# Eight shared-expert tasks in front of the routed tasks, none among them

## The chip, the cores and the metric

The kernel runs on one core of a Trainium2 chip. The metric is the time of one execution on the device in microseconds (us); the median of three runs is given. Matrix products run on TensorE (PE), elementwise work on VectorE (DVE), activations and copies on ScalarE (ACT), small operations and gathers and scatters by index on GpSimd (POOL), and most plain transfers are issued by SyncE (SP) and ScalarE.

## What is computed

One transformer layer over a batch of two sequences of 1,024 tokens, width 256: attention and then a mixture of experts, each behind a layer norm and with a residual.

```python
x = x + attention(layernorm(x))          # 16 heads of 128, causal
x = x + ffn(layernorm(x))

def ffn(x):                              # 2,048 tokens
    topk_idx, topk_w = route(x)          # sigmoid scores; 4 of 8 groups, 8 of 32 experts
    for g, u, d, c in 32 experts:        # inner size 128
        out += c[:, None] * ((silu(x @ g.T) * (x @ u.T)) @ d.T)
    shared = (silu(x @ shared_gate.T) * (x @ shared_up.T)) @ shared_down.T    # inner size 256
    return out + shared
```

Each token uses 8 of the 32 routed experts, and every token uses the shared one.

## The kernel before

The first 940 us are attention, for both sequences (batch 0 and batch 1), in head pairs; while the second half of it runs, the tokens of batch 0 are normalized and routed, and their rows are written to a buffer `xs` in device memory, sorted by expert, in tiles of 128 rows. Every expert gets at least one tile; each batch has room for 96 tiles, and tiles behind the last used one are computed as tiles of the last expert in the order. Products are split into three of reduced precision each (a high and a low part; lines 824 to 826, helper `three`).

The experts' work is a fixed list of 112 **tasks**, built by `dealt()`. A *routed* task ("m") is two tiles of sorted rows, 48 for each batch (routed tasks 0 to 47 are batch 0, from 48 on batch 1); a *shared* task ("s") is 128 tokens through the shared expert, 8 for each batch. Before the change the order is: shared 0 to 3 of batch 0, routed 0 to 26, shared 4, routed 27 to 34, shared 5, routed 35 to 42, shared 6, routed 43 to 50, shared 7, routed 51 to 95, and the 8 shared tasks of batch 1. A task's position in the list is called g. So routed task 27 stands at g = 32, 40 at 46, 42 at 48, 52 at 60; from routed task 51 on, g is the task's number plus 8.

All engines go through the same list of items, written by `step_items(n)`. Step n is: A, the gate and up products of task n + 2 (`gate_up`, 12 products a task, lines 824 to 826); E, if task n + 4 is routed, the transposes of its rows (`transpose_rows`, L1016); B, the transposes of the hidden values of task n + 1 (L1028); C, the down products of task n (`down`, L1047). A shared task has no E: its rows are the tokens, which are in SBUF already, and its weights are there too. TensorE handles the items in exactly this order, so an A that waits holds everything behind it.

The first 36 steps (`after_attention`) also hold batch 1's second normalization half (items N, and the transposes Y), the router's logits (L, M), routing (G) and slots (K), two to a step for the first 20 steps and one after that, put in at places 1 and 3 of each step's list. An E that isn't there moves what is behind it one place forward.

Weights of the routed experts come through a **ring** of 8 places. SyncE loads expert e (512 KB of split gate and up weights, 128 KB of down weights) into place e mod 8 as soon as the tiles of expert e - 8 have been computed:

```python
if e >= RING:
    until_done(0, e - RING)      # waits on s_y, which counts computed tiles
load(e % RING, e, wanted)        # two transfers, L569 and L570
if e > 0:
    relay(0, e - 1)              # L565: waits for e - 1 to land, then s_w += 1
```

An expert between 8 and 23 without tokens is skipped. TensorE's `gate_up` waits until `s_w` says that the weights of the task's second tile are there. Batch 1 goes through the experts in reverse order, 31 first, and starts with the eight that batch 0 left in the ring; its first new load needs its own first tile computed.

Other transfers in this stretch: ScalarE loads the sorted rows, 512 KB for two routed tasks, four pairs ahead, and stores the results of two tasks in the same way (512 KB). GpSimd scatters the rows of batch 1 to their sorted places: 64 scatters of 128 rows of 1 KB, of which scatter i waits for task g = 15 + i // 2 to be done; then it gathers result rows for batch 0 and 1, in 128 gathers, each pair behind one more task (from g = 47 on). These gates go by the position g, not by the routed task's number. VectorE adds a shared task's output to the tokens' sum (L1592) and splits off low parts (L1595 for rows, L1344 for normalized tokens); the rows of a token are added with their weights from step 62 on.

Of the kernel before, what the change touches and what calls it, by code (L numbers as in the profile page):

```python
# [97 lines left out]
NEWTON = range(NC, B * NC + 2)  # L98
NS = B * NT
NTASK = NS + B * PT  # L100
LEAD, DEALT_BEHIND = 4, (26, 34, 42, 50)
NSH = SI // I
TAIL = 36
COMBINE = NT + PT + 6
# [1620 lines left out]
```

## Time and profile before

| | |
|---|---|
| median of 3 runs | 1325.95 us (1322.28 to 1327.79) |
| the profiled execution | 1325.1 us, of which the span from first to last instruction is 1323.4 |
| instructions | 28,678 |
| TensorE busy in the span | 1285.6 us (97%) |
| VectorE, ScalarE, GpSimd busy | 884.5, 736.3, 571.5 us |
| mean granted TensorE clock | 0.994 of full speed |
| start of the first shared task's gate-up | 944.5 us |

Times in the rows are counted from the start of the span. A profile's timeline merges like instructions that follow each other: "1.03 PE L1047 ... x4" are four products that take 1.03 us from the first one's start to the last one's end. What stands in brackets behind a row is the engine's idle time just before it and what ended it. Matmuls overlap, so the time of a step is best read from start to start.

### The profile page before, as it was taken

How to read it: one execution, taken by the hardware profiler on the slowest of the kernel's cores; microseconds unless marked ns; L12 is line 12 of the kernel's file. 1: busy time of each engine (PE TensorE's matmuls, PEld its weight loads, DVE VectorE, ACT ScalarE, POOL GpSimd, SP SyncE). 2: the span in 40 equal slices, each digit the busy share in tenths (PEclk: the TensorE clock that was granted, in tenths of full speed). 3: DMA queues.
4: the chain of work that ended last, by engine and by line, in shares of the span. 5: the costliest groups of instructions: out<-in, count | busy, mean ns of one | idle time of the engine just before them, and what ended most of it. 6: DMA issues, size and time to landing. Idle time of an engine off the chain costs nothing.

```text
span 1323.4 us, 28678 instructions
## 1 busy us (share of the span) xinstructions
PE 1285.6 (97%) x8324; PEld 1154.0 (87%) x8324; DVE 884.5 (67%) x2120; ACT 736.3 (56%) x1660; POOL 571.5 (43%) x675
## 2 busy tenths in 40 slices
PE   7999999999999999999999999999999998999998
PEld 6898888988888897879888888988789998899996
DVE  5666666776766969687777766676767532356645
ACT  3656555565555655455555555555556664566653
POOL 3636445364430414132244537363000764666674
PEclk8999999999999999999999999999999999999999
DMA  3252645525362001010001112011268998999973
GB/s 125 88 183 89 208 135 182 184 97 182 122 222 99 18 16 29 5 28 19 19 29 61 44 62 69 26 51 57 64 223 290 305 318 297 316 317 389 366 236 115
DMA packets 124796, 188.18 MB, mean 142 GB/s; under 512 B 10016, under 2 KB 97824, under 8 KB 124704
## 3 DMA queue, kind: packets, MB, share of 16 engines
q1 hardware_dynamic: 61024, 101.91, 23.2%
q10 hardware_dynamic: 51392, 51.52, 11.9%
q0 software_dynamic: 12288, 33.57, 7.3%
q8 instruction: 52, 0.85, 0.3%
q14 instruction: 40, 0.33, 0.1%
HBM read 107.79 MB, written 87.03 MB: 147 GB/s over the span
## 4 chain that ended last, share of the span: by engine, by line
PE 79%; DVE 7%; issue 7%; ACT 4%; DMA 3%; SPq 0%; ACTq 0%; POOL 0%; DVEq 0%; POOLq 0%
PE ps_t L879 8%; PE ps_s L824 7%; PE ps_s L826 7%; PE ps_s L825 7%; PE ps_x L824 6%; PE ps_x L826 5%; PE ps_x L825 5%; PE ps_z L824 4%; PE ps_z L826 4%; PE ps_z L825 4%; PE ps_t L1047 3%; PE ps_z L1047 3%; PE ps_s L1016 3%; PE ps_t L824 2%; PE ps_t L826 2%
## 5 line engine op out<-in xcount | busy, mean ns | idle before, releaser
L1170 ACT ACTIVATE prob<-prob,neg_max 128x128 f32<-128x128 f32 (+7 forms) x256 | 198.6, 776 | 244.0 <-DVE neg_max L1370 243.8
L1391 DVE TENSOR_TENSOR pT_lo<-ps_t,pT_hi 128x512 fp32r<-128x512 f32 (+2 forms) x320 | 189.8, 604 | 101.3 <-ACT pT_hi L1185 98.7
L1185 ACT ACTIVATE pT_hi<-ps_t 128x512 fp32r<-128x512 f32 (+2 forms) x320 | 161.5, 532 | 86.3 <-PE ps_t L879 86.3
L1370 DVE CUSTOM_DVE_ANT_0 prob<-ps_s,later_keys 128x128 f32<-128x128 f32 (+7 forms) x256 | 186.1, 749 | 1.9 <-PE ps_s L826 0.8
L879 PE MATMUL ps_t<-ident,prob 128*128 128x128 f32 x1152 | 170.9, 273 | 8.1 <-ACT prob L1170 6.0
L719 POOL DMA_INDIRECT xs<-xn,slots x128 | 125.5, 981 | 123.0 <-DVE slots L1538 53.3
L879 PEld LDWEIGHTS ps_t<-ident,prob 128*128 128x128 f32 x1152 | 136.5, 140 | 33.4 <-issue 6.1
L824 PE MATMUL ps_s<-k_hi,q_hi 128*128 128x512 f32 (+2 forms) x384 | 140.9, 367 | 0.9 <-DVE k_lo L1363 0.9
L1583 DVE TENSOR_TENSOR h<-sg,ps_s 128x256 f32<-128x256 f32 x112 | 47.1, 421 | 137.2 <-ACT sg L1219 137.0
L824 PE MATMUL ps_s<-ring,a_hi 128*128 x384 | 126.4, 329 | 7.3 <-SPq L565 7.0
L634 POOL TENSOR_TENSOR a_hi<-raw_a,zero 128x512 fp32r<-128x512 f32 x30 | 31.2, 1040 | 236.0 <-PE ps_x L826 194.3
L826 PE MATMUL ps_s<-k_hi,q_lo 128*128 128x512 f32 (+2 forms) x384 | 131.9, 344 | 0.0
L825 PE MATMUL ps_s<-k_lo,q_hi 128*128 128x512 f32 (+2 forms) x384 | 131.6, 343 | 0.0
L824 PE MATMUL ps_z<-pT_hi,v_hi 128*128 128x512 f32 (+2 forms) x320 | 122.5, 383 | 1.6 <-DVE pT_lo L1391 1.6
L826 PE MATMUL ps_z<-pT_hi,v_lo 128*128 128x512 f32 (+2 forms) x320 | 115.7, 361 | 0.0
L825 PE MATMUL ps_z<-pT_lo,v_hi 128*128 128x512 f32 (+2 forms) x320 | 114.9, 359 | 0.0
L826 PE MATMUL ps_s<-ring,a_lo 128*128 x384 | 109.5, 285 | 0.0
L1406 DVE SCALAR_TENSOR_TENSOR acc<-ps_t,inv_sum,acc 128x256 f32<-128x256 f32 x256 | 108.7, 477 | 0.2 <-PE ps_t L826 0.2
L825 PE MATMUL ps_s<-ring,a_hi 128*128 x384 | 108.5, 282 | 0.0
L1219 ACT ACTIVATE sg<-ps_s 128x256 f32<-128x256 f32 x112 | 43.1, 385 | 113.9 <-PE ps_s L826 113.8
L1363 DVE TENSOR_TENSOR k_lo<-ps_x,k_hi 128x512 fp32r<-128x512 f32 x62 | 42.9, 691 | 66.1 <-ACT k_hi L1163 66.0
L824 PEld LDWEIGHTS ps_s<-ring,a_hi 128*128 128x128 f32 x384 | 72.9, 190 | 11.7 <-issue 9.3
(304 smaller groups left out, 3535.0 us busy)
## 6 DMA issues: line engine op xcount, KB each, us to landing
ring<-ws SPq DMA_DIRECT2D x56, 512.0 KB, 4.3
xs<-taken SPq DMA_DIRECT2D x16, 1536.0 KB, 9.7
xq<-xs ACTq DMA_DIRECT2D x48, 512.0 KB, 4.8
xs<-yq ACTq DMA_DIRECT2D x48, 512.0 KB
ws<-split_to SPq DMA_DIRECT2D x34, 512.0 KB, 3.1
raw<-experts_dram SPq DMA_DIRECT2D x34, 256.0 KB, 3.4
raw_a<-w_a_dram SPq DMA_DIRECT2D x15, 512.0 KB, 3.8
ring_down<-experts_dram SPq DMA_DIRECT2D x56, 128.0 KB, 5.8
```

The lines of the kernel that those rows point to most:

```text
L719: pool.indirect_dma_start(xs[b], bass.IndirectOffsetOnAxis(ap=slots[b][:, t, k:k + 1], axis=0), xn[:, t, :], None).then_inc(s_xs[b], 16)
L824: pe.matmul(to, w_hi, m_hi, start=start, stop=False, skip_group_check=joins)
L825: pe.matmul(to, w_hi, m_lo, start=False, stop=False, skip_group_check=joins)
L826: return pe.matmul(to, w_lo, m_hi, start=False, stop=stop, skip_group_check=joins)
L879: last = pe.transpose(bank[:, j * P:(j + 1) * P], prob[c][:, j, n * P:(n + 1) * P], ident[:, :])
L1047: last = pe.matmul(to, hT[g % 2][:, at], downs[g][j], start=what == "m" or j == 0, stop=what == "m" or j == 1)
L1170: act.activation(to, to, ACT.Exp, scale=-1.0, bias=neg_max[:, r:r + 1], accum_out=row_sum[:, c, j:j + 1]).then_inc(s_exp, 1)
L1185: act.activation(pT_hi[t % 3][:, j * P:], ps_t[m % 2][:, j * P:], ACT.Copy).then_inc(s_hi, 1)
L1370: dve.tensor_tensor_reduce(prob[r // BC][:, r % BC, 0:width(r)], ps_s[r % 2][:, first:first + width(r)], later_keys[:, S - width(r):], 1.0 ...
L1391: dve.tensor_tensor(lo, ps_t[m % 2][:, j * P:], hi.bitcast(F32), ALU.subtract).then_inc(s_bank_free, 1)
L1406: last = dve.scalar_tensor_tensor(to, ps_t[m % 2][:, j * D:(j + 1) * D], inv_sum[:, c, q:q + 1], to, ALU.mult, ALU.add)
L1583: dve.tensor_tensor(by[0], by[1], ps_gu[g % 2].rearrange("p (j m i) -> p j m i", j=2, m=2)[:, :, 1], ALU.mult).then_inc(s_h, 1)
```

## The change

Two constants are changed. `LEAD` is the number of shared tasks of batch 0 in front of the first routed task, `DEALT_BEHIND` the routed tasks behind which one of the others stands.

```diff
-LEAD, DEALT_BEHIND = 4, (26, 34, 42, 50)
+LEAD, DEALT_BEHIND = 8, ()
```

After it the order is: shared 0 to 7 of batch 0, routed 0 to 95, the shared tasks of batch 1. Every routed task stands at g = number + 8: routed tasks 0 to 26 four places later than before, 27 to 34 three, 35 to 42 two, 43 to 50 one, and from 51 on at the same place. Tasks, items, transfers and their sizes are the same ones. The gates of the scatters and gathers and the items woven into the first steps stay at the same g. The first four steps now have no E, and the steps ahead of the former places of shared tasks 4 to 7 have one.

## Rows read from the trace of the kernel before

**Rows 1.** Page, part 1: busy time, share of the span, instructions.
```profile
PE 1285.6 (97%) x8324; PEld 1154.0 (87%) x8324; DVE 884.5 (67%) x2120; ACT 736.3 (56%) x1660; POOL 571.5 (43%) x675
```

**Rows 2.** Waits of TensorE, 980 to 1324 us: total, times, longest.
```profile
PE ps_s L824 <- SPq L565: 7.0, 4, 2.5
PE ps_s L1121 <- DMA yg<-xs,slots: 1.0, 1, 1.0
```

**Rows 3.** Timeline of TensorE: gate-ups 29 to 32 (start, length, instruction).
```profile
1053.32 0.47 PE L824 MATMUL ps_s<-ring,a_hi 128*128 x1
...
1055.84 0.47 PE L824 MATMUL ps_s<-ring,a_hi 128*128 x1
...
1058.80 0.47 PE L824 MATMUL ps_s<-shared_gu,xT_hi 128*128 128x256 f32 x1
...
1061.69 0.47 PE L824 MATMUL ps_s<-ring,a_hi 128*128 x1
```

**Rows 4.** Timeline of TensorE: gate-ups 45, 46, 47, 48 and 50.
```profile
1099.64 0.47 PE L824 MATMUL ps_s<-ring,a_hi 128*128 x1
...
1105.41 0.38 PE L824 MATMUL ps_s<-ring,a_hi 128*128 x1 [2.46 <-SPq L565]
...
1111.85 0.38 PE L824 MATMUL ps_s<-ring,a_hi 128*128 x1 [1.66 <-SPq L565]
...
1115.04 0.38 PE L824 MATMUL ps_s<-ring,a_hi 128*128 x1 [0.39 <-SPq L565]
...
1120.80 0.47 PE L824 MATMUL ps_s<-ring,a_hi 128*128 x1
```

**Rows 5.** Timeline of TensorE: gate-ups 59, 60 and 61.
```profile
1146.92 0.47 PE L824 MATMUL ps_s<-ring,a_hi 128*128 x1
...
1152.73 0.38 PE L824 MATMUL ps_s<-ring,a_hi 128*128 x1 [2.50 <-SPq L565]
...
1157.20 0.47 PE L824 MATMUL ps_s<-ring,a_hi 128*128 x1
```

**Rows 6.** Timeline of SyncE: loads of experts 23 and 31, first one of batch 1.
```profile
1077.08 0.33 SPq L569 DMA_DIRECT2D ring<-ws  x1
...
1109.79 0.33 SPq L569 DMA_DIRECT2D ring<-ws  x1
...
1144.20 0.34 SPq L569 DMA_DIRECT2D ring<-ws  x1
```

**Rows 7.** Waits of SyncE's queue: before 1077.2, 1077 to 1116, before 1144.3.
```profile
SPq L569 <- PE ps_t L1047: 12.1, 1, 12.1
...
SPq L565 <- DMA ring_down<-experts_dram: 22.7, 9, 3.3
...
SPq L569 <- PE ps_z L1047: 27.9, 1, 27.9
```

**Rows 8.** Windows: length, busy time (instructions) by engine, PEclk, DMA share, GB/s.
```profile
1077.00:1105.40 28.40, 25.95 (x193) 24.67 (x191) 9.76 (x19) 16.00 (x35) 19.14 (x20) 1.00 1.01 368
...
1144.00:1152.70 8.70, 6.23 (x46) 5.64 (x44) 2.88 (x5) 4.51 (x10) 6.62 (x7) 1.00 0.95 320
...
1153.50:1155.00 1.50, 1.50 (x9) 1.50 (x9) 0.00 (x0) 0.00 (x0) 0.00 (x0) 0.51 1.09 353
```

**Rows 9.** Timelines of VectorE and TensorE in the first steps.
```profile
972.45 0.73 DVE L1338 TENSOR_SCALAR xn<-acc,mv,scale 128x256 f32<-128x256 f32 x2
...
975.09 0.66 PE L832 MATMUL ps_x<-ident,xn 128*128 128x128 f32 x4 [1.09 <-DVE xT_lo L1344]
```

**Rows 10.** Timeline of GpSimd: first and last of 26 scatters, of seven gathers.
```profile
1077.11 0.96 POOL L719 DMA_INDIRECT xs<-xn,slots  x1 [0.73 <-PE ps_t L1047]
...
1119.80 0.96 POOL L719 DMA_INDIRECT xs<-xn,slots  x1 [0.30 <-issue]
...
1144.04 0.95 POOL L790 DMA_INDIRECT yg<-xs,slots  x1 [0.30 <-issue]
...
1151.75 0.95 POOL L790 DMA_INDIRECT yg<-xs,slots  x1 [0.30 <-issue]
```

## The prediction

> **What bounds the kernel.** I read the page first, then the waits of TensorE, then the timelines of TensorE, SyncE's queue and GpSimd around those waits, and last the table of windows. The page says that TensorE is the bound [rows 1]. The change touches only the last 380 us, in which the experts' tasks run. From 980 us on, TensorE's waits are short: 7.0 us in four waits for SyncE's relay of the weight ring (L565), and the next largest of the list is 1.0 us [rows 2]. So this stretch is TensorE work, plus four ring waits. The order of tasks can't change the amount of work; it can change only what stands between a ring load's trigger and the task that needs it.
>
> The step length is read from the starts of consecutive gate-ups. A routed task takes 2.96 us (1055.84 to 1058.80), a shared one 2.89 (1058.80 to 1061.69), and a step whose fourth task ahead is shared has no row transposes and takes 2.52 (1053.32 to 1055.84) [rows 3]. The transposes are 2.96 - 2.52 = 0.44, so a shared task costs 2.89 - 0.44 = 2.45 us wherever TensorE is busy.
>
> The four ring waits are at gate-ups 46, 47, 48 and 60, that is at routed tasks 40, 41, 42 and 52: they start at 1105.41, 1111.85, 1115.04 and 1152.73 with idle times of 2.46, 1.66, 0.39 and 2.50 us before them [rows 4, 5].
>
> What each waits for is the ring. By the code, SyncE loads expert e when the tiles of expert e - 8 are done, then waits until e - 1 has landed before it goes on, so two loads are in flight. It waited 12.1 us for TensorE until 1077.08 (expert 23, behind the down product of routed task 29) and after that, until expert 31 at 1109.79, it waited for landings: nine waits, 22.7 us [rows 6, 7]. So nine loads run as a chain from routed task 29: 1077.08 to 1115.04 is 38.0 us, 4.2 us a load, with the DMA engines 101% busy at 368 GB/s [rows 8]. By the order of the relays (each let one of them start) task 40 needs expert 28, task 41 expert 30, task 42 expert 31. In the second place SyncE waited 27.9 us for routed task 48, the first of batch 1, and issued the first new load of batch 1 at 1144.20 [rows 6, 7]; routed task 52 was released by it at 1152.73, 8.5 us later [rows 5].
>
> **The change, part by part.** Nothing is added or removed. Of the moved tasks, that behind 26 lies before both triggers in either order: 0. That behind 34 lies inside the first chain, that behind 42 just behind its end, that behind 50 between task 48 and task 52. Take the start of the same routed task in both kernels, and follow its shift.
>
> 1. Down product of routed task 29, which starts the chain. Three shared tasks more stand ahead of it: 3 x 2.45 = +7.35.
>
> 2. The front. There, batch 1's normalization is woven in. TensorE waits for the normalized rows (VectorE, from 972.45) and then 1.09 us for their low part, a VectorE operation too, until 975.09 [rows 9]. The first three steps now lack their row transposes, 3 x 0.44 = 1.3 us, which stood in this gap and ahead of it. VectorE's chain is set by its own work: the normalized rows come at the same time, the low part hardly earlier (a split operation less ahead of it, but ScalarE's high part comes first). I take 0.2 to 0.3 us earlier of 1.3: +1.1 of new idle. From both sides: -0.3 (VectorE's freed time lets the chain end earlier) and +1.5 (all cover lost). In all +8.45 at task 29.
>
> 3. The chain. Its cover shrinks by a shared task, but it ends where the DMA engines let it end, so the release of task 42 moves with task 29. What the chain shares the engines with: row loads and stores go with routed tasks and are the same; GpSimd's scatters go with the position in the list. Behind 1077.08 GpSimd issued 26 scatters, the last at 1119.80, of which 23 before 1115.04 [rows 10]. With positions three higher at task 29, 20 are left there. Three scatters of 128 rows of 1 KB are 0.39 MB, at 368 GB/s 1.1 us: -1.1. From both sides: 0 (slots that a scatter leaves are filled by other rows) and -4.0 (nine loads at 3.8 us). Task 42: +7.35. That the two terms meet is chance.
>
> 4. Behind the chain. Gate-up 48 to gate-up 50 was 1115.04 to 1120.80, 5.76 us with the shared task between them [rows 4]; without it 2.96: -2.80. Task 43: +4.55.
>
> 5. The step that lacked its transposes for the task behind 50 is now a whole one: +0.44. Task 48, second trigger: +4.99.
>
> 6. The load for task 52. Trigger to release was 8.5 us [rows 5, 6]. TensorE's work inside shrinks by 2.89, so its idle grows to about 4 us, but the release moves with the trigger. GpSimd issued seven gathers from 1144.04 to 1151.75 [rows 10], because it had fallen behind its gates; in the new order its scatters end earlier against the tasks, so it is at its gates, and with TensorE standing at task 52 four are issued: 3 x 0.13 MB at the 320 GB/s of this stretch [rows 8] is 1.2 us: -1.2. From both sides: 0, and -3.2, if it takes only the 5.3 us of expert 31's load (1109.79 to 1115.04 [rows 4, 6]). Task 52: +3.8.
>
> 7. The clock. Behind the wait of 2.50 us the granted clock was 0.51 between 1153.5 and 1155 [rows 8], that is the level of 1.2 GHz, and gate-up 60 to 61 took 4.47 us in place of 2.96 [rows 5], 1.5 lost. With a longer idle ahead of it, I take +0.3; from both sides 0 and +1.5 (one more such step).
> Here the Trainium skill, "TensorE: Matmul & The Clock Gate", section "Loop structure matters more than you think", speaks against the change: a long wait for a DMA between matmuls makes TensorE go cold. The trace agrees in two of four waits (2.46 and 2.50 us, not 1.66 and 0.39), and by that rule both the old and the new order pay at task 52, so it adds nothing but what step 7 has.
>
> From task 52 on TensorE doesn't wait before the last microseconds, so the shift stays to the end. Sum: 8.45 - 1.1 - 2.80 + 0.44 - 1.2 + 0.3 = +4.1 us. On the profiled execution (1325.1, of which the span is 1323.4 and 1.7 lie around it) that is 1329.2; it lay 0.85 below the median of the three runs, 1325.95, so the predicted median is 1330.0 us.
>
> Said in another way: a shared task was worth its cover in two places, behind 34 and behind 50, some 5.0 us together; transfers that thin out give back 2.3, the front costs 1.1 and the clock 0.3.
>
> **Rivals.**
> *The transfers take it all back.* If the chain and the load of task 52 are a matter of bytes per second, a TensorE that stands still issues no row traffic, and the loads hurry. For it: expert 31's load, issued with TensorE just released, was used after 5.3 us (1109.79 to 1115.04 [rows 4, 6]), against 8.4 in the chain (two in flight, 4.2 each). Against it: in both orders TensorE stands in the last part only, and the same rows must pass. Price: chain -3.0 and load -3.2 in place of -1.1 and -1.2, so +0.2: 1326.2.
> The Trainium skill, "DMA: Bandwidth & Descriptors", section "Issuing engines are not separate DMA queues", says that transfers started by SyncE, ScalarE and GpSimd interleave on the same 16 engines. The 101% of this stretch agrees, and it is this rule that makes the rival possible.
>
> *The load for task 52 gets slower* (the other side). By the code ScalarE asks for the rows of routed tasks 60 and 61 when it handles the rows of task 53. With the shared task gone, that comes some 3 us sooner after the trigger, and its 512 KB stand beside the ring load: 0.52 MB at 320 GB/s is 1.6 us, and the relief of 1.2 is lost. Price +2.8: +6.9, 1332.9. It decides if trigger to release takes 9.8 us or more (8.5 before, 7.3 in my sum). Against it: no landing of the chain took that long.
>
> *The waits go away.* If the scatters, and not the bytes, made the loads slow, all four waits and the slow step would go. Gate-ups 45 to 50 took 21.16 us [rows 4], of 14.29 without waits (three of 2.96, one of 2.52, one of 2.89); so 6.9 less, and at task 52 the wait of 2.85 (1152.73 less 1146.92 + 2.96 [rows 5]) and the slow step's 1.5, 11.2 in all, plus 1.1 at the front: 1315.9. Against it: 20 of 23 scatters stay in the chain.
>
> **Chances.** The sum's way 0.60, all taken back 0.19, slower load 0.16, no waits 0.03, something else 0.02. What a measurement of this kernel can tell from no change is about 0.5%, 6.6 us: 1319.3 to 1332.6. The first two cases lie inside; the sum's own bounds reach to +8 (0.03 of its weight goes over the upper edge). So faster 0.03, same 0.79, slower 0.18. Bounds of the sum: low -0.3 + 7.35 - 4.0 - 2.8 + 0.44 - 3.2 = -2.5, high 1.5 + 7.35 - 2.8 + 0.44 + 1.5 = +8.0; all terms at one end together are unlikely, so the range is 1325.0 to 1333.8, which leaves the "no waits" case and the outer ends out.
>
> **What would show it.** Four ring waits at the same routed tasks 40, 41, 42 and 52 (now gate-ups 48, 49, 50 and 60), that before 40 some 1.5 us longer (or a small one before 39), that before 52 near 4 us instead of 2.5; the trigger of expert 23 some 8.5 us later, and 36.9 us from there to task 42; an idle time near 2 us in the front at the second transposes of batch 1's normalized rows; first new load of batch 1 some 5 us later. I am wrong if the chain from task 29 gets shorter by 3 us or more, if a new ring wait shows up before task 38, or if TensorE waits in the routing of batch 1 (positions 6 to 20), where VectorE now has four additions of shared outputs more.

## The result, and the profile after

| | before | after |
|---|---|---|
| median | 1323.71 us (5 runs, 1322.28 to 1327.79) | 1330.86 us (5 runs, 1328.97 to 1332.82) |
| ratio | | 1.0047 (95% interval 1.0030 to 1.0064) |
| span of the profiled execution | 1323.4 us | 1327.2 us |

The changed kernel is slower by 6.2 us by the ratio, with an interval from 4.0 to 8.5. That is just inside the 0.5% that the prediction gave as the bound of what can be told from no change, but the interval lies above zero. The prediction was 1330.0 us (+4.1), range 1325.0 to 1333.8; it started from the median of three runs, 1325.95, which with five runs is 1323.71.

In the waits of TensorE from 940 us on (total us, times, longest), the relay of the ring is still the first, now with 11.4 us in place of 7.0 [rows 2]:

```profile
PE ps_s L824 <- SPq L565: 11.4, 4, 5.8
PE ps_x L832 <- DVE xn L1338: 1.3, 2, 0.6
PE ps_x L832 <- DVE xT_lo L1344: 1.2, 1, 1.2
```

TensorE's timeline, gate-ups of routed tasks 39 to 43 (positions 47 to 51) and of 51 to 53 (positions 59 to 61), to be read beside [rows 4, 5]:

```profile
1103.77 0.47 PE L824 MATMUL ps_s<-ring,a_hi 128*128 x1
...
1111.32 0.57 PE L824 MATMUL ps_s<-ring,a_hi 128*128 x1 [4.24 <-SPq L565]
...
1117.80 0.38 PE L824 MATMUL ps_s<-ring,a_hi 128*128 x1 [1.03 <-SPq L565]
...
1121.38 0.38 PE L824 MATMUL ps_s<-ring,a_hi 128*128 x1 [0.34 <-SPq L565]
...
1124.27 0.47 PE L824 MATMUL ps_s<-ring,a_hi 128*128 x1
...
1147.95 0.47 PE L824 MATMUL ps_s<-ring,a_hi 128*128 x1
...
1157.02 0.58 PE L824 MATMUL ps_s<-ring,a_hi 128*128 x1 [5.76 <-SPq L565]
...
1161.47 0.47 PE L824 MATMUL ps_s<-ring,a_hi 128*128 x1
```

The waits are before the same four routed tasks, 40, 41, 42 and 52, and no new one is there. That before 40 grew from 2.46 to 4.24 us, that before 52 from 2.50 to 5.76.

SyncE's loads of expert 23 and 31 and the first new one of batch 1, beside [rows 6]:

```profile
1083.66 0.33 SPq L569 DMA_DIRECT2D ring<-ws  x1
...
1116.37 0.33 SPq L569 DMA_DIRECT2D ring<-ws  x1
...
1148.11 0.34 SPq L569 DMA_DIRECT2D ring<-ws  x1
```

From the first one to the gate-up of task 42 it is 37.7 us (38.0 before). The load for task 52 is issued at 1148.11 and releases it at 1157.02, 8.9 us later (8.5 before). The windows of these two stretches, and of the step behind the second (columns as in [rows 8]):

```profile
1083.66:1121.38 37.72, 32.12 (x219) 29.93 (x218) 11.14 (x21) 18.64 (x41) 19.19 (x20) 0.91 0.99 356
1148.10:1157.00 8.90, 3.16 (x23) 2.68 (x22) 1.58 (x3) 2.47 (x6) 3.78 (x4) 0.82 0.99 318
1157.50:1161.50 4.00, 4.00 (x23) 3.92 (x22) 0.52 (x2) 1.11 (x3) 0.00 (x0) 0.62 0.09 33
```

In the chain the DMA engines are full (0.99) at nearly the rate of before (356 GB/s; 360 from 1077.08 to 1115.04 before), with 20 GpSimd instructions in it (23 before), and between trigger and release of task 52 there are four. The granted clock of 0.91 in the chain is that of the step behind the wait before task 40; it costs little, since task 41 has to wait anyway.

**A measure for the comparisons.** The attention part differs between two executions by a microsecond or so that has nothing to do with the order of tasks (gate-up 2 starts at 965.44 in the profile before and 964.03 in the one after). So below I use the stretch from the start of gate-up 2 to that of gate-up 103, the last routed task; it holds the same tasks in all kernels. It is 315.6 us before and 321.1 after, +5.4. The changed kernel's ratio of 1.0047 rests on five runs, those of the experiments on 6 to 12 each.

### The profile page after: what moved, and what is told of

Its sections match the earlier page's. It is cut to its first block, busy times and chain, and to the rows that moved or that the text cites. A ratio compares the mean times of both kernels' runs of the same rounds, so it can differ in the third digit from the quotient of the medians.

```text
span 1327.2 us, 28678 instructions
## 1 busy us (share of the span) xinstructions
PE 1284.7 (97%) x8324; PEld 1153.0 (87%) x8324; DVE 884.4 (67%) x2120; ACT 736.3 (55%) x1660; POOL 571.4 (43%) x675
## 4 chain that ended last, share of the span: by engine, by line
PE 78%; issue 7%; DVE 6%; ACT 4%; DMA 3%; SPq 0%; ACTq 0%; POOL 0%; DVEq 0%; POOLq 0%
PE ps_t L879 8%; PE ps_s L824 7%; PE ps_s L826 7%; PE ps_s L825 7%; PE ps_x L824 6%; PE ps_x L826 6%; PE ps_x L825 5%; PE ps_z L824 4%; PE ps_z L826 4%; PE ps_z L825 4%; PE ps_t L1047 3%; PE ps_z L1047 3%; PE ps_s L1016 3%; DMA ring_down<-experts_dram 3%; PE ps_t L824 2%
## 5 line engine op out<-in xcount | busy, mean ns | idle before, releaser
L824 PE MATMUL ps_s<-k_hi,q_hi 128*128 128x512 f32 (+2 forms) x384 | 140.6, 366 | 0.9 <-DVE k_lo L1363 0.9
L824 PE MATMUL ps_s<-ring,a_hi 128*128 x384 | 126.7, 330 | 11.4 <-SPq L565 11.4
L825 PE MATMUL ps_s<-k_lo,q_hi 128*128 128x512 f32 (+2 forms) x384 | 131.4, 342 | 0.0
L824 PE MATMUL ps_z<-pT_hi,v_hi 128*128 128x512 f32 (+2 forms) x320 | 122.5, 383 | 1.6 <-DVE pT_lo L1391 1.6
L825 PE MATMUL ps_z<-pT_lo,v_hi 128*128 128x512 f32 (+2 forms) x320 | 114.9, 359 | 0.0
L825 PE MATMUL ps_s<-ring,a_hi 128*128 x384 | 109.0, 284 | 0.0
L824 PEld LDWEIGHTS ps_s<-ring,a_hi 128*128 128x128 f32 x384 | 73.5, 192 | 15.6 <-issue 13.3
```

What stands on the lines that cost most here:

```text
L824: pe.matmul(to, w_hi, m_hi, start=start, stop=False, skip_group_check=joins)
L825: pe.matmul(to, w_hi, m_lo, start=False, stop=False, skip_group_check=joins)
```

## The experiments

Each kernel is the changed one with the edit shown, or names another base. Ratios are to the kernel before.

**1. Only the task behind 50 goes back.**

```diff
-LEAD, DEALT_BEHIND = 8, ()
+LEAD, DEALT_BEHIND = 7, (50,)
```

> The changed kernel, but the eighth shared task stands behind routed task 50 again (LEAD 7, DEALT_BEHIND (50,)). Measure: gate-up 2 to gate-up 103 in TensorE's timeline, 315.6 us before the change, 321.1 after. Theory of the lost cover: the wait before routed task 52 is back near 2.5 us (5.8 after the change) and the stretch is 2.9 us shorter than after, 318.2; time about 1.0022 of the kernel before. Rival (the place of the task is no matter, the load lengthens or shortens with it): wait stays above 4.5 us, stretch 320.5 to 321.5.

Ratio 1.0018 (1.0004 to 1.0032), where the sum had about 1.0022. In the profile the wait before task 52 is short again:

```profile
1157.12 0.42 PE L824 MATMUL ps_s<-ring,a_hi 128*128 x1 [2.90 <-SPq L565]
```

But the stretch of this one profile was 321.75 us and not 318.2: the chain took 39.7 us in place of 37.7, and 1.6 us were lost in the front, of which more below. The lost cover behind 50 is shown by its own wait, by the timed runs here and by those of experiment 3; one profile's stretch alone would have spoken against it.

**2. Only one behind 34.**

```diff
-LEAD, DEALT_BEHIND = 8, ()
+LEAD, DEALT_BEHIND = 7, (34,)
```

> The changed kernel, but the eighth shared task stands behind routed task 34 again (LEAD 7, DEALT_BEHIND (34,)). Theory of the lost cover: the wait before routed task 40 falls from 4.2 us to near 2; TensorE's work ahead of the chain of loads is 2.45 us less, the chain stays 37.7 to 38 us long, and the stretch from gate-up 2 to 103 is 318.6 us (321.1 after the change). The wait before task 52 stays at 5.8. Rival (the chain is a matter of how much work and traffic lies in it, so it lengthens with the task in it): chain over 39.5 us, stretch 320.5 or more.

Ratio 1.0028 (1.0013 to 1.0042): 2.5 us less than the changed kernel, but the two intervals overlap. The waits before tasks 40 and 41, from TensorE's timeline:

```profile
1110.97 0.38 PE L824 MATMUL ps_s<-ring,a_hi 128*128 x1 [1.85 <-SPq L565]
...
1117.46 0.58 PE L824 MATMUL ps_s<-ring,a_hi 128*128 x1 [3.27 <-SPq L565]
```

The wait before 40 fell from 4.24 us to 1.85, near the 2 expected, but that before 41 grew from 1.03 to 3.27. The chain's waits together are 5.1 us, 5.6 in the changed kernel and 4.5 in the kernel before. So most of what left the first wait came back in the second, in this profile.

The chain was 38.6 us, between the theory's and the rival's number but nearer to the first. The stretch, 320.7, again has the 1.6 us of the front in it. The wait before task 52 was 3.95 us, not 5.8: the load took 7.1 us in this execution.

**3. Both.**

```diff
-LEAD, DEALT_BEHIND = 8, ()
+LEAD, DEALT_BEHIND = 6, (34, 50)
```

> Six shared tasks in front, one behind routed task 34 and one behind 50 (LEAD 6, DEALT_BEHIND (34, 50)). Theory: those behind 26 and 42 never covered anything, so the waits are those of the kernel before (2.5, 1.7, 0.4 and 2.5 us), and the stretch from gate-up 2 to 103 is that of before, 315.6, plus what two missing row transposes leave idle in the first steps, 0.5: 316.1. Rival (each of the four was worth a quarter of the loss of 5.4): 318.3.

Ratio 1.0001 (0.9989 to 1.0013). The two positions 34 and 50 together give the loss back, to within 1.6 us; those behind 26 and 42 are worth nothing that can be measured. The mean is 2.7 us (about +- 1.8) under that of experiment 2, which lacks only the task behind 50, and 1.7 us (about +- 2.1) under that of experiment 1, which lacks only that behind 34. So the share of 50 is clear of the noise, and that of 34 alone is not. The waits were not those of the kernel before, as expected, but 1.69 us before 40, 4.03 before 41 and 2.94 before 52. (The one profile had a stretch of 321.5, with a chain of 40.2 us and the 1.6 us in front; the timed runs decide.)

**4. The front: same change, another order in its first four steps.**

```diff
-            for at in (1, 3) if n < 20 else (2,):
+            for at in (1, 3 + (n < 4)) if n < 20 else (2,):
```

> The changed kernel with another order in its first four steps: the second woven item stands behind the down products and not ahead of them, where the missing row transposes had stood. That puts 0.68 us of work into the 1.2 us wait for the normalized rows' low part. In five of seven profiles with six or more shared tasks in front the clock fell to half behind this wait (3.4 us at half, 1.6 lost), in none of the three with four. Theory (the wait brings the clock down): wait 0.5, clock 1.00 from 973 to 979, gate-up 2 to 8 takes 22.0 us (22.6 and 22.7 in the changed kernel's two profiles, 24.2 in the one whose clock fell), time 1 to 2 us under the changed kernel, 1.003 to 1.004 of before. Rival (it is chance, with no tie to this wait): the clock falls again, 23.7 or more.

This was made because of what the profiles above showed. With six or more shared tasks in front, TensorE waits twice for the normalized rows, 0.65 us for the rows and then 1.20 (0.97 in one kernel) for their low part; with four in front there is only the second wait, 1.09 [rows 9]. In five of the seven profiles with both waits the clock then fell. Windows 973 to 979 us (the third number from the end is the granted clock), of a kernel whose clock fell (experiment 6 below) and of the changed one, whose clock didn't:

```profile
973.00:975.00 2.00, 0.81 (x6) 0.57 (x7) 1.21 (x3) 0.87 (x2) 0.00 (x0) 0.96 0.94 283
975.00:977.00 2.00, 2.00 (x8) 1.73 (x7) 0.69 (x1) 0.60 (x1) 0.00 (x0) 0.50 0.71 250
977.00:979.00 2.00, 2.00 (x13) 1.91 (x13) 0.42 (x1) 0.00 (x0) 0.00 (x0) 0.69 0.84 271
```

```profile
973.00:975.00 2.00, 1.42 (x9) 1.32 (x10) 0.62 (x2) 0.67 (x2) 0.00 (x0) 1.00 0.91 297
975.00:977.00 2.00, 2.00 (x17) 1.79 (x16) 0.96 (x3) 0.45 (x2) 0.00 (x0) 1.00 0.87 292
977.00:979.00 2.00, 2.00 (x11) 1.45 (x10) 0.39 (x1) 1.97 (x3) 0.00 (x0) 1.00 0.61 202
```

Both have the same two waits. The second of them, and the products behind it, in the timeline of the first kernel:

```profile
974.65 0.97 PE L832 MATMUL ps_x<-ident,xn 128*128 128x128 f32 x4 [1.20 <-DVE xT_lo L1344]
975.42 1.91 PE L1047 MATMUL ps_t<-shared_down,hT 128*128 128x256 f32 x4
```

where four down products take 1.91 us and not 1.03. With the other order the two waits are 0.31 and 0.33 us:

```profile
973.38 0.65 PE L832 MATMUL ps_x<-ident,xn 128*128 128x128 f32 x2 [0.31 <-DVE xn L1338]
...
975.44 0.66 PE L832 MATMUL ps_x<-ident,xn 128*128 128x128 f32 x4 [0.33 <-DVE xT_lo L1344]
```

Gate-up 2 to 8 took 21.5 us (22.6 and 22.7 in the changed kernel's two profiles, 24.2 in experiments 6 and 7, which have its order of tasks and whose clock fell), and the clock stayed at 1.00. So the profile shows that the waits in the front cost 1.1 us, 2.7 where the clock falls, and that the edit takes them back. The ratio is 1.0025 (1.0014 to 1.0036), 2.9 us under the changed kernel where 1 to 2 were expected; but experiments 2, 6 and 7, whose front still has both waits, came down as far (1.0028, 1.0029 and 1.0029), so the timed runs don't single out the front. That the clock falls because of these waits fits all profiles, but one profile with it at 1.00 can't prove it, since two with the waits had it too.

**5. The changed kernel and the one before, once more.**

> The changed kernel once more, unchanged, for a second profile: how far the chain (expert 23's load to gate-up of routed task 42, 37.7 us in the first profile) and the load for task 52 (8.9 us) vary from one execution to the next. Theory: both depend on how the transfers interleave, so they differ by 1 to 2 us. Rival: they repeat to 0.3 us, and the 39.7 us of e1_keep50, which has the same tasks in the chain, comes from the gates that stand one place later.

> The kernel before once more, unchanged. Theory: gate-up 2 to 8 takes 23.4 us with the clock at 1.00, the chain from expert 23's load to gate-up of routed task 42 is 38.0 +- 1, release of task 41 34.8 +- 1, load to release of task 52 8.5 +- 0.7 us. Rival (the clock falls in the front of this kernel too): 25.0.

| us | before | before again | after | after again |
|---|---|---|---|---|
| gate-up 2 to 103 | 315.6 | 317.3 | 321.1 | 320.3 |
| chain, expert 23's load to task 42 | 38.0 | 39.6 | 37.7 | 38.0 |
| of it, to task 41 | 34.8 | 35.8 | 34.1 | 33.9 |
| load for task 52 to its release | 8.5 | 8.2 | 8.9 | 7.5 |
| gate-up 2 to 8 | 23.4 | 23.5 | 22.6 | 22.7 |

Where TensorE neither waits nor runs at half clock its steps repeat to 0.1 us; the two stretches that hang on transfers vary by up to 1.6 us. The chain of the kernel before, 39.6, is outside its expected 38.0 +- 1; that of the changed kernel repeated to 0.3 us, its load for task 52 only to 1.4. The one further run of the changed kernel took 1328.50 us, 4.3 over the median of the kernel before that was timed with it (1324.19); the medians of experiments 6 and 7, timed with it too, are 1328.90 and 1328.98. So the terms of the transfers have to be read over all profiles. With two loads in flight and the scatters' gates unchanged: the chain is 38.5 us in the mean of four without a shared task in it (37.7, 38.0, 38.5 and 39.7 in the changed kernel, twice, and experiments 4 and 1), 39.1 in the mean of four with one (38.0, 39.6, 38.6, 40.2). The load for task 52 is 7.6 us in the mean of six in which no shared task is behind 50 (8.9, 7.5, 6.6, 7.1, 7.7, 7.8), 8.7 in four with one (8.5, 8.2, 9.0, 9.0). For the chain the two groups overlap, and 0.6 us between their means is less than the spread inside either.

**6. Fewer scatters in the chain.**

```diff
-SCATTER_FROM, GATHER_FROM = 15, 15 + NT * TOPK // 2
+SCATTER_FROM, GATHER_FROM = 7, 15 + NT * TOPK // 2
```

> The changed kernel, with the scatters' gates eight tasks earlier (SCATTER_FROM 7 in place of 15), so that GpSimd scatters as fast as it can and is done near 1102 us: some 15 scatters lie behind the load of expert 23 in place of 20. Theory of bytes (my -1.1 for three scatters): the chain from the load of expert 23 to gate-up of routed task 42 is 37.7 - 1.8 = 35.9 us, the stretch from gate-up 2 to 103 is 319.3 (321.1 in the changed kernel). Rival (the engines' time is filled by something else, scatters don't matter): 37.7 +- 1. Rival (scatters of small rows slow every load beside them): under 34.

The chain was 37.0 us, 1.5 under the mean of 38.5, and 33.7 to task 41 where the two profiles of the changed kernel have 34.1 and 33.9. The theory had 1.8 less than 37.7. The sign and the size fit the bytes, but 0.8 to 1.5 us is no more than what the chain varies by. The rival that small rows slow every load (under 34) is out. Ratio 1.0029 (1.0018 to 1.0041), 2.4 us under the changed kernel with intervals that overlap; the stretch of the profile, 321.5, holds the fallen clock of the front.

**7. Three loads in flight.**

```diff
-            if e > 0:
-                relay(0, e - 1)
+            if e > 1:
+                relay(0, e - 2)
+        relay(0, E - 2)
         relay(0, E - 1)
```

> The changed kernel, but in batch 0 SyncE relays expert e - 2 and not e - 1 after it has issued the load of e, so three ring loads are in flight in place of two. Theory of bytes (the chain is set by what the 16 engines move): chain from expert 23's load to gate-up of routed task 42 stays within 1.5 us of 37.7; the waits before 40 and 41 may swap sizes. Rival (two loads in flight are too few, each takes its 8 us whatever else moves): 9 loads take two thirds, 26 to 30 us, the waits before 40 to 42 go, and the stretch from gate-up 2 to 103 falls from 321.1 by 6 us or more.

In between. Task 41 was released 31.1 us after expert 23's load (34 with two), and the wait before 40 is gone; to task 42 it was 36.0. SyncE's loads of experts 23 to 26 came at a pace of 2.7 us, not 3.6 as in the changed kernel:

```profile
1085.27 0.33 SPq L569 DMA_DIRECT2D ring<-ws  x1
...
1089.30 0.34 SPq L569 DMA_DIRECT2D ring<-ws  x1
...
1091.87 0.33 SPq L569 DMA_DIRECT2D ring<-ws  x1
...
1093.39 0.33 SPq L569 DMA_DIRECT2D ring<-ws  x1
```

But the later relay made TensorE wait before tasks 32 and 33 (1.47 and 0.72 us; the two steps took 4.78 and 3.93 us), which it had not. Ratio 1.0029 (1.0020 to 1.0039). The rival, a chain of 30 us or less, is out: most of the chain is not due to the two loads at a time. Whether some 3 us of it are, this one profile can't tell. Experiment 11 has three in flight as well, and there task 41 was released 34.9 us after expert 23's load, as with two in flight in the kernel before (34.8 and 35.8).

**8. The four tasks where the waits are.** (This and the next three are edits of the kernel before.)

```diff
-LEAD, DEALT_BEHIND = 4, (26, 34, 42, 50)
+LEAD, DEALT_BEHIND = 4, (34, 38, 49, 50)
```

> Four shared tasks in front, and the other four where the ring waits are: behind routed tasks 34 and 38 (both inside the chain of loads) and behind 49 and 50 (both between the first new load of batch 1 and its first user). Theory of the cover: against the kernel before, one more covers the chain, -2.45, and one more covers the load for task 52, whose wait of 2.85 us and the slow step behind it (1.5) go: 315.6 - 6.8 = 308.8 us from gate-up 2 to 103, time 0.995 of before. Waits before tasks 40 to 42 about 2.4 us shorter in sum, none before 52. Rival (the loads are a matter of bytes, and each shared task inside brings two scatters or gathers more and stretches them): no more than -2 us, 313.6 or more.

Ratio 0.9988 (0.9979 to 0.9997), stretch 314.2 us: far less than the 6.8 expected. The second half came as expected: no wait before task 52, and gate-up of task 48 to that of 53 took 21.6 us before and 19.7 here with one shared task more inside, so 4.3 less net. The first half gave nothing, and there was a new wait:

```profile
PE ps_s L824 <- SPq L565: 4.8, 1, 4.8
PE ps_t L1028 <- ACT hT L1229: 2.1, 1, 2.1
```

ScalarE asks for the first rows of batch 1 at the rows of routed task 45 and waits there for all scatters, with hT behind it. The scatters' gates go by position; the routed tasks had moved forward against them.

**9. The same, scatters four tasks earlier.**

```diff
-LEAD, DEALT_BEHIND = 4, (26, 34, 42, 50)
+LEAD, DEALT_BEHIND = 4, (34, 38, 49, 50)
-SCATTER_FROM, GATHER_FROM = 15, 15 + NT * TOPK // 2
+SCATTER_FROM, GATHER_FROM = 11, 15 + NT * TOPK // 2
```

> The order of e4_cover (shared tasks behind routed 34, 38, 49 and 50) with the scatters' gates four tasks earlier (SCATTER_FROM 11). In e4_cover, ScalarE's load of batch 1's first rows waited for the last scatter and held hT back: TensorE stood 2.14 us, the step took 5.51 in place of 2.96. Theory: that wait goes, and the stretch from gate-up 2 to 103 is 314.2 - 2.6 = 311.6; time about 0.9965 of the kernel before. Rival (the ring chain has to end first anyway, so what is gained there is waited for elsewhere): 314.2, 0.9988.

Ratio 0.9976 (0.9967 to 0.9985), stretch 312.8 us: that wait is gone, and half of what was expected came. In the chain a single wait is left, and a step of 4.97 us behind it:

```profile
1112.16 0.58 PE L824 MATMUL ps_s<-ring,a_hi 128*128 x1 [5.01 <-SPq L565]
...
1117.13 0.47 PE L824 MATMUL ps_s<-ring,a_hi 128*128 x1
```

From expert 23's load to task 41 it was 36.3 us with two shared tasks inside (36.1 in experiment 8; 34.2 to 35.8 in four profiles with one, 33.9 to 35.9 in four with none), and to task 42 41.3. With the second task in it the chain is longer by more than a microsecond, with the first one it isn't clear of the spread; and the slow step, which before was hidden in the chain (it ran before task 41, which waited anyway), stands behind it.

**10. Cover and three loads in flight.** Experiment 9 with the edit of 7.

> e7_cover_gates (shared tasks behind routed 34, 38, 49 and 50, scatters four tasks earlier) with three ring loads in flight in batch 0. In e7 one wait of 5.0 us is left, before routed task 41, with a slow step behind it (4.97 us). With three in flight (e6) task 41 was released 31.1 us after the load of expert 23, 34.1 with two. Theory: that takes 3 us of the wait and, if under some 2.5 us are left, the slow step too: stretch from gate-up 2 to 103 is 312.8 - 3 to 5 = 307.8 to 309.8, time 0.994 of the kernel before. Rival (the chain is bytes, and with both covers in it there is nothing to gain): 312 or more, 0.9976.

Ratio 0.9953 (0.9938 to 0.9969): 1317.95 us against 1324.17, the fastest of all. The stretch is 309.5 us, at the edge of what the theory had. What is left of waits for the ring is 3.7 us in three, two of them the late relays' before tasks 32 and 33. (The edit of 7 adds a line, so L825 here is L824 elsewhere.)

```profile
PE ps_s L825 <- SPq L565: 3.7, 3, 1.5
```

**11. With one task in the chain in place of two.** Experiment 10 with `DEALT_BEHIND = (26, 34, 49, 50)`.

> e9_cover_three with the shared task behind routed 26 in place of 38, so only one shared task lies in the chain. Tells what the second cover in the chain is worth. Theory of the cover: 2.45 us less work there, the wait longer by as much: stretch 2.4 us longer than in e9. Rival (as between before and e7, where the second cover bought nothing: the chain grew by 1.5 us and the slow step came out from under it): within 0.7 us of e9.

Ratio 0.9976 (0.9967 to 0.9985), stretch 312.4 us: 2.8 us more than in 10. With three loads in flight the second cover is worth its full 2.45 us and a little more. With two it seems to have bought nothing: the task behind 49 alone gave 4.3 us in the profile of experiment 8, and experiment 9, which has both, is 3.2 us under the kernel before by its ratio. Experiment 11 has the same ratio with three in flight and no second cover, so three in flight by itself seems to have bought nothing either. No kernel has two in flight, one task in the chain and one behind 49, so these two readings are argued from sums, and only the step from experiment 11 to 10 is shown.

## Why the prediction was right

**Where the time goes** was right. That the loss sits at the two positions 34 and 50 and not at 26 and 42 is shown by experiment 3; that behind 50 is clear in the timed runs by itself (experiments 1 and 3), that behind 34 has the expected sign and size in experiments 2 and 3, each time within the noise, and the front is shown in the profiles (experiment 4).

**Point by point**, shifts against the kernel before, counted from gate-up 2 in the first two profiles:

| step | predicted | measured |
|---|---|---|
| 1, three tasks ahead of task 29 | +7.35 | with 2: 7.98, of which 7.35 is work |
| 2, the front | +1.1 | +1.2; 1.6 more where the clock falls |
| 3, the chain | -1.1 | -0.2 in the pair, -0.6 over the means |
| 4, no task behind 42 | -2.80 | -2.87 |
| 5, a whole step | +0.44 | +0.42 |
| 6, the load for task 52 | -1.2 | +0.4 in the pair, -1.1 over the means |
| 7, the slow step | +0.3 | 0.0 in the pair (4.45 us after, 4.47 before), +0.2 over the means |
| sum | +4.1 | +5.4 in the pair, 4.2 in the mean of two pairs |

How the first lines are worked out: task 29 starts at 1074.17 - 964.03 = 110.14 after gate-up 2, before at 1067.60 - 965.44 = 102.16. Gate-up 8 comes 0.86 us earlier against gate-up 2 (22.57 and 23.43), where the work alone would make it 2.04 earlier (four transposes of 0.44 and four shared gate-ups of 0.07), so 1.2 are idle. The rest, -0.55, came in one step, 19, that of a routing operation whose successor found TensorE waiting for 0.3 us less; I had nothing on it. The measured terms of the pair add to 5.7; the 42 steps behind task 53 took 123.6 us in place of 123.9, which makes the 5.4.

**What was mis-sized.** Step 2 took the front as idle time only. In five of seven profiles with six or more shared tasks in front its waits were followed by half clock, 1.6 us each. At that share it is 1.1 us more, and with the 4.2 of the means it makes 5.3, against 6.2 (4.0 to 8.5) measured. (The mean granted clock of the timed runs, 0.990 to 0.992 after and 0.994 in the profile before, says that more time was at half clock, but not where.) Step 3 took 1.1 us off the chain for three scatters, and 0.6 over the means is within the spread. Step 7 charged a longer wait with a longer slow step. In the pair the step didn't change (4.5 us after 2.5 and after 5.8 us of waiting), but over ten profiles it took 4.3 to 5.4 us, and not by the length of the wait: 5.35 after 2.94 us, 4.48 after 4.34. The steps of 5.2 to 5.4 us ran at a granted clock of 0.50 to 0.52, those of 4.3 to 4.5 us at 0.60 to 0.66. The six without a shared task behind 50 have a mean of 4.9, the four with one 4.6. Step 6's four gathers were there; that its relief was not in the first pair but in the mean shows that a term of 1 us on transfers can't be read from two profiles.

**What was luck.** The predicted 1330.0 us lies 0.9 under the measured 1330.86 because the median that it started from was 2.2 us high; from 1323.71 the sum of +4.1 gives 1327.8. The 4.2 us of the two pairs is so near to 4.1 because neither changed profile has the fallen clock in front, and because the 0.55 us of step 19, which the sum lacked, makes up in part for a relief of the transfers that came out smaller.

**The rivals.** *The transfers take it all back* would have needed 35.0 us for the chain and 5.3 for the load; with two loads in flight and the gates unchanged the shortest chain was 37.7, and the shortest of ten loads for task 52 6.6. *The load for task 52 gets slower* has its point at 9.8 us: the longest was 9.0, and these were kernels with the shared task behind 50 in place. *The waits go away* had no sign; they grew. The rule of the Trainium skill ("TensorE: Matmul & The Clock Gate", "Loop structure matters more than you think"), that a long wait for a DMA makes TensorE go cold, agrees with task 52: behind all ten waits there, of 2.1 to 5.8 us, the granted clock of the next step was 0.50 to 0.66. In the front no DMA was waited for, and yet the clock fell in five of seven profiles behind 0.65 and 1.20 us (0.97 in one) of waiting for VectorE; that was my omission.

What stays open: why the chain took 39.7 us in experiment 1 and 37.7 with the same tasks in it in the changed kernel. I take it for the interleaving of the queues; it was not isolated. Open as well are why the half clock lasted through the slow step in four profiles and ended within it in six, and 0.2 of the 0.55 us of step 19, where the shorter wait accounts for 0.3.

## What to carry to other kernels

Work that needs no transfer is worth up to its length where it stands between a load's trigger and a user that waits for the load, and here nothing measurable elsewhere: so find trigger and user of each wait before moving it, and check what else moves with it (gates that count positions, and waits that were covered by accident in the first steps). In a chain of loads that is paced by its transfers, a second such task seems to have only moved the wait; together with a third load in flight its gain came (0.9953 against 0.9976). And moving under 1% of the work gives differences of the size by which transfers vary from run to run: decide with the timed runs, and use the profile for the place.

## What the runs showed of the hardware

- A wait of 2.1 to 5.8 us before the gate-up of task 52 was followed by a slow step of 4.3 to 5.4 us against 2.96, in ten profiles of ten, at a granted clock of 0.50 to 0.66; the longer wait did not go with the longer step (4.45 us after 5.76, 5.35 after 2.94).
- Two waits of 0.65 and 1.20 us (0.97 in one), 0.9 us of work between them, were followed by a stretch at 1.2 GHz in five profiles of seven; with 0.31 and 0.33 us it didn't come in one. What stood between the waits were transposes.
- A ring load of 640 KB takes 6.6 to 9.0 us from issue to release beside the same row traffic, and the mean falls from 8.7 to 7.6 us with three gathers and a shared task less beside it (four profiles and six).
